# Perceiver block: pairs of batches for the last channels, one S step, and the tail column by DMA

## The reference

```
q, k, v = x@Wq, ctx@Wk, ctx@Wv           # 8 heads of 64
x += softmax(q k^T / 8) v @ Wo + bo      # over the 257 context rows of the batch
w = sigmoid(xn@Wx@Ww + bw); k, v, r = xn@Wk, xn@Wv, sigmoid(xn@Wr)
state_t = (1 - w_t) state_{t-1} + k_t v_t^T;  out_t = r_t state_t   # 4 heads, 32 steps
x += out @ Wo
x += gelu(xn@U1@V1 + b1) @ U2 @ V2 + b2
```

## Time and profile before

| | |
|---|---|
| median of 3 runs | 970.15 us (969.84 to 971.87) |
| profiled execution | 969.11 us, span 967.1 us |
| PE busy | 943.9 us (98%) |
| ACT, DVE, POOL busy | 607.3, 613.0, 373.8 us |
| DMA | 79.03 MB, mean 82 GB/s |

### The profile page before, as it was taken

The page is one execution under the profiler, slowest core; times in us unless marked ns, Lnnn a source line. Parts: engine busy times, 40 slices in busy tenths (PEclk is TensorE's granted clock), DMA queues, the critical chain, the costliest instruction groups (busy, mean ns, idle before and its releaser), DMA issues.

```text
span 967.1 us, 23520 instructions
## 1 busy us (share of the span) xinstructions
PE 943.9 (98%) x9012; PEld 783.6 (81%) x9012; DVE 613.0 (63%) x1286; ACT 607.3 (63%) x1487; POOL 373.8 (39%) x484
## 2 busy tenths in 40 slices
PE   9999999999999999999999999999999999999998
PEld 7767888787888878798887878888787888877775
DVE  4765858476685847668485666747567584746461
ACT  3545657667575766767576675757757566674533
POOL 1423534244352524435253352524326252433330
PEclk9999999999999999999999999999999999999999
DMA  8314231322323132132222313122222313222000
GB/s 304 120 51 124 59 105 49 100 81 65 105 78 90 51 101 81 60 110 61 88 69 87 95 60 94 60 87 89 81 80 81 90 49 89 87 73 72 9 12 22
DMA packets 58013, 79.03 MB, mean 82 GB/s; under 512 B 10288, under 2 KB 39856, under 8 KB 57904
## 3 DMA queue, kind: packets, MB, share of 16 engines
q1 hardware_dynamic: 56192, 76.38, 25.9%
q10 hardware_dynamic: 1712, 1.16, 0.4%
HBM read 73.05 MB, written 4.46 MB: 80 GB/s over the span
## 4 chain that ended last, share of the span: by engine, by line
PE 78%; DVE 9%; ACT 7%; issue 3%; POOL 1%; DMA 0%; DVEq 0%; POOLq 0%; ACTq 0%
PE gb L369 16%; PE scores L428 7%; PE acc L459 7%; PE gb L492 6%; PE acc L455 6%; PE scores L432 6%; PE ptp L442 5%; PE acc L460 5%; PE gb L613 3%; PE gb L602 3%; DVE xn L840 3%; ACT probs L685 3%; PE gb L401 3%; DVE probs L853 2%; DVE small L846 2%
## 5 line engine op out<-in xcount | busy, mean ns | idle before, releaser
L1100 POOL TENSOR_TENSOR t_l<-raw_t,t_h 128x516 fp32r<-128x516 f32 x128 | 167.5, 1309 | 193.6 <-PE scores L432 131.0
L685 ACT ACTIVATE probs<-scores,small 128x257 f32<-128x257 f32 x256 | 119.1, 471 | 134.6 <-DVE small L846 134.4
L846 DVE TENSOR_REDUCE small<-scores 128x2 f32<-128x514 f32 x128 | 88.3, 690 | 127.5 <-PE scores L432 127.4
L1109 POOL TENSOR_TENSOR ptm<-probs,head 128x32 f32<-128x32 f32 x128 | 35.1, 274 | 261.9 <-DVE probs L853 261.9
L853 DVE TENSOR_TENSOR probs<-probs,small 128x514 f32<-128x514 f32 x128 | 101.7, 794 | 4.4
L459 PE MATMUL acc<-pt,raw_n 128*128 128x256 f32 x256 | 89.6, 431 | 0.0
L442 PE MATMUL ptp<-ident,probs 128*128 128x128 f32 x512 | 78.7, 276 | 10.5 <-DVE probs L853 9.4
L696 ACT ACTIVATE pt<-ptp 128x512 f32<-128x512 f32 x128 | 77.2, 603 | 13.2 <-PE ptp L442 11.7
L455 PE MATMUL acc<-pt,raw_n 128*64 128x128 f32 x1024 | 82.7, 282 | 2.3 <-ACT pt L696 0.4
L428 PE MATMUL scores<-t_h,qk_h 128*128 128x258 f32 x256 | 83.3, 325 | 0.0
L455 PEld LDWEIGHTS acc<-pt,raw_n 128*64 128x64 f32 x1024 | 55.4, 136 | 31.9 <-issue 21.0
(11 more groups left out here) (178 smaller groups left out, 2768.8 us busy)
## 6 DMA issues: line engine op xcount, KB each, us to landing
raw_t<-in_ctx_t SPq DMA_DIRECT2D x128, 258.0 KB, 3.3
raw_n<-in_ctx_n SPq DMA_DIRECT2D x128, 192.0 KB, 2.4
xb<-in_x SPq DMA_DIRECT2D x16, 256.0 KB, 4.3
vsp<-tail_values SPq DMA_DIRECT2D x256, 2.0 KB
out<-ob SPq DMA_DIRECT2D x16, 256.0 KB, 2.9
xin<-in_x SPq DMA_DIRECT2D x15, 256.0 KB, 2.9
khat<-in_wq ACTq DMA_DIRECT2D x1, 512.0 KB, 4.3
wv<-in_wv SPq DMA_DIRECT2D x1, 512.0 KB, 6.3
```

Of the source, the lines that this page charges most:

```text
L685: go(probs[n % 2][:, r, 0:L], scores[:, r, 0:L], ACT.Exp, bias=nmax[:, r:r + 1], accum_out=rsum[:, r:r + 1]).then_inc(s["exp_ready"], 1)
L846: v_.tensor_reduce(nmax[:], scores[:, :, 0:L], AX.X, ALU.max, negate=True)\
L1100: p_.tensor_tensor(t_l[m % 2][:], raw_t[m % RING][:], t_h[m % 2][:].bitcast(F32), ALU.subtract)\
```

## The change

- pv: the 64-channel products of a batch are done by table RESTS: those of batches 2 and 3 both at b=3, 4 and 5 at b=5, 6 and 7 at b=7. At b=2, 4, 6 only L459 and L460 are left. The transposed probabilities of the first of each pair wait in `xn0`'s memory (`pt_late`), so step xn0 waits for the group's last sums. `pc_out` copies 256 columns for such a batch and 128 more for its partner. `raw_n` loads of a pair come together.
- Tail column: POOL's `ptm`, PE's TP and DVE's `psp` product go. SP moves the last column of each half by a DMA (128 numbers on 128 partitions to 4 rows of 32) into one of two zeroed `psp`, so two DMAs a batch; ACT's exps wait for those of two batches before. Half of the `vsp` DMAs go.
- S is one step with two tiles at b=7 instead of two steps with four; DVE has two masks of twice the size, behind `norm_probs`.
- Order of the fills: Qf from b=0 to b=7 (same group, one batch earlier), H from b=7 to b=6, Pf from b=6 to b=4, v from b=6 to b=5, Y3 from b=1 to b=2.

```diff
-FILL1 = [["Sq", "Qf", "WV"], ["O2"], [], ["Qa0"], ["Qa1"], ["Qb"], [], ["Sp", "H0", "H2"]]
-FILL2 = [["St"], ["Y3", "Y1", "XT"], ["Y2", "XT2", "q0", "q2"], ["z", "q1", "q3", "XT3"], ["k"], ["r"], ["Pf", "v"],
-         ["TP"]]
+FILL1 = [["WV"], ["O2"], [], ["Qa0"], ["Qa1"], ["Qb"], ["H0", "H2"], ["S", "Qf"]]
+FILL2 = [["St"], ["Y1", "XT"], ["Y3", "Y2", "XT2", "q0", "q2"], ["z", "q1", "q3", "XT3"], ["k", "Pf"], ["r", "v"], [],
+         []]
+RESTS = [[0], [1], [], [2, 3], [], [4, 5], [], [6, 7]]
...
-SHIFT = {"XT": PREP, "TP": HERE}
+TILES.update({"S": ["S0", "S1"], "St": ["St0", "St1"]})
+SHIFT = {"XT": PREP}
 SHIFT.update({f"q{p}": PREP for p in range(4)})
 SHIFT.update({n: PREP for n in ("Qa0", "Qa1", "Qb")})
-SHIFT.update({n: POST for n in "WV Y1 XT2 z k r v Sp".split()})
-SHIFT.update({n: FFN for n in "Sq St O2 Y2 XT3 Pf H0 H2".split()})
-SHIFT.update({n: END for n in ("Qf", "Y3")})
+SHIFT.update({n: POST for n in "WV Y1 XT2 z k r v S".split()})
+SHIFT.update({n: FFN for n in "St O2 Y2 XT3 Pf H0 H2 Qf".split()})
+SHIFT["Y3"] = END
...
+def rests(n):
+    return [n - n % G + b for b in RESTS[n % G]]
+def sums(n):
+    return sum(1 + 2 * len(rests(m)) for m in range(n + 1))
...
+        pt_late = xn0[:].rearrange("p t d -> p (t d)").rearrange("p (t m) -> p t m", t=LT)
...
+        def pt_of(n):
+            return pt if n in rests(n) else pt_late
...
+                    step = n - RING
+                    while n - RING not in rests(step):
+                        step += 1
+                    sp.wait_ge(s["acc_ready"], sums(step))
...
-                    for half in range(2):
-                        sp.dma_start(vsp[half * 64 + h:half * 64 + 64:H, cols], scratch[g * G:(g + 1) * G, cols])\
-                            .then_inc(vsp_in, 16)
+                    half = h // 4
+                    sp.dma_start(vsp[half * 64 + h:half * 64 + 64:H, cols], scratch[g * G:(g + 1) * G, cols])\
+                        .then_inc(vsp_in, 16)
...
+            def tail_column(n):
+                g, b = n // G, n % G
+                if n == 0:
+                    sp.wait_ge(s["psp_ready"], 1)
+                sp.wait_ge(s["probs_ready"], n + 1)
+                if b == 0 and g > 1:
+                    bank, k = BANK["WV1", g - 2]
+                    sp.wait_ge(bank_filled[bank], k)
+                for r in range(2):
+                    row = 64 * r + H * b + 4 * r
+                    sp.dma_start(psp[g % 2][row:row + 4, b], probs[n % 2][:, r, L - 1:L]).then_inc(tail_in[n % 2], 16)
...
+                for m in rests(n):
+                    c0 = P * (n - m)
+                    for t in range(LT):
+                        for k in range(2):
+                            last = mm(acc[64 * k:64 * k + 64, 1, c0:c0 + P], raw_n[m % RING][:, t, P:C],
+                                      pt_of(m)[:, t, k * P:(k + 1) * P], start=t == 0, stop=t == 1)
+                            if t == 1:
+                                last.then_inc(s["acc_ready"], 1)
+                x, p_ = raw_n[n % RING], pt_of(n)
+                mm(acc[:, 0], x[:, 0, 0:P], p_[:, 0], start=True, stop=False)
+                mm(acc[:, 0], x[:, 1, 0:P], p_[:, 1], start=False, stop=True).then_inc(s["acc_ready"], 1)
...
+            def s_tiles(g):
+                even, odd = (tile(n, g)[:].rearrange("p a (c k) -> p (a c) k", k=P) for n in ("S0", "S1"))
                 pe.wait_ge(s["hat_ready"], HATS * (g + 1))
                 pe.wait_ge(s["rhat_ready"], 2 * (g + 1))
                 for t in range(2):
-                    t_ = slice(t * P, (t + 1) * P)
-                    for i in range(NB):
-                        keys = i * 2 * T + c * T + t * P
-                        queries = i * 2 * T // NB + (2 * c + t) * 32
-                        for r0, out_ in ((0, even), (64, odd)):
-                            last = mm(out_[32 * i:32 * i + 32, 0, t_],
-                                      rhat[r0:r0 + 64, queries:queries + 32],
-                                      khat[r0:r0 + 64, keys:keys + P], start=True, stop=True)
-                            if (t, i) == (1, NB - 1):
-                                done(f"S{2 * c + r0 // 64}", g, last)
+                    for c in range(2):
+                        for i in range(NB):
+                            keys = i * 2 * T + c * T + t * P
+                            queries = i * 2 * T // NB + (2 * c + t) * 32
+                            for r0, out_ in ((0, even), (64, odd)):
+                                last = mm(out_[32 * i:32 * i + 32, 2 * t + c], rhat[r0:r0 + 64, queries:queries + 32],
+                                          khat[r0:r0 + 64, keys:keys + P], start=True, stop=True)
+                                if (t, c, i) == (1, 1, NB - 1):
+                                    done(f"S{r0 // 64}", g, last)
...
-                    act.wait_ge(s["ptm_ready"], n - 1)
+                    act.wait_ge(tail_in[n % 2], 32 * (n // 2))
...
+                act.wait_ge(s["acc_ready"], sums(n))
+                b, own = n % G, n in rests(n)
+                if len(rests(n)) > 1:
+                    go(pc[:, H:, (b - 1) * S:b * S], acc[:, 1, P:2 * P].rearrange("p (h s) -> p h s", s=S), ACT.Copy)
+                columns = H + H // 2 if own else H
+                go(pc[:, 0:columns, b * S:(b + 1) * S],
+                   acc[:].rearrange("p c (h s) -> p (c h) s", h=H)[:, 0:columns], ACT.Copy)\
...
-                    drain(n, g, v_.copy_predicated(s_q[:, 2 * c + e:2 * c + e + 5:4],
-                                                   mask[:].rearrange("p (o q) -> p o q", o=1).to_broadcast([P, 2, P]),
-                                                   t[:, 0].rearrange("p (t q) -> p t q", t=2)))
+                    drain(n, g, v_.copy_predicated(s_q[:, int(n[1])::2],
+                                                   mask[:].rearrange("p (o q) -> p o q", o=1).to_broadcast([P, 4, P]),
+                                                   t[:].rearrange("p a (c q) -> p (a c) q", q=P)))
...
-            GAPS = [[["psp-1"], ["S2-2", "S3-2"], ["WV0-1", "WV1-1"]],
-                    [[], [], ["O2-2", "Y3-3", "Y1-1"]],
-                    [["XT+1", "xn1-1"], [], []],
+            GAPS = [[[], [], ["WV0-1", "WV1-1"]],
+                    [[], [], ["O2-2", "Y1-1"]],
+                    [["XT+1", "xn1-1"], [], ["Y3-3"]],
                     [["Y2-2"], ["XT2-1", "xn2-2"], ["Qa0+1"]],
                     [[], ["su-1"], ["Qa1+1", "ti-1", "i0-1"]],
-                    [[], ["cf-1"], ["Qb+1", "i1-1"]],
-                    [[], ["i2-1", "pr-1"], ["rh-1", "ln0+2"]],
-                    [[], ["S0-1", "S1-1"], ["xn0+2"]]]
-            AT_END = [[[["psp-1"], ["S2-2", "S3-2"], ["WV0-1", "WV1-1"]],
+                    [[], ["cf-1"], ["Qb+1", "i1-1", "i2-1"]],
+                    [[], ["pr-1"], ["rh-1", "ln0+2"]],
+                    [[], [], ["S0-1", "S1-1", "xn0+2"]]]
```

More of the change, by code:

```diff
@@ L181, in build @@
         pc = sb("pc", [P, H + H // 2, T])
-        ptm = [sb(f"ptm{i}", [P, 2, 2, G, H]) for i in range(2)]
-        psp = sb("psp", [P, G, S])
-        ones = psp[:].rearrange("p b s -> p (b s)")
+        psp = [sb(f"psp{i}", [P, G, S]) for i in range(2)]
+        zeros = psp[1][:].rearrange("p b s -> p (b s)")
         vsp = sb("vsp", [P, INNER])
         xin, xn0 = sb("xin", [P, 2, D]), sb("xn0", [P, 2, D])
+        pt_late = xn0[:].rearrange("p t d -> p (t d)").rearrange("p (t m) -> p t m", t=LT)
         hid = sb("hid", [P, 8, T])
@@ L250, in build @@
                              "out_done"))
+        tail_in = [sem(f"tail_in{i}") for i in range(2)]
         ctxt_in = [sem(f"ctxt_in{i}") for i in range(RING)]
@@ L450, in pv @@
                     pe.wait_ge(s["pc_ready"], n)
-                x = raw_n[n % RING]
-                for t in range(LT):
-                    for k in range(2):
-                        last = mm(acc[64 * k:64 * k + 64, 1, 0:P], x[:, t, P:C], pt[:, t, k * P:(k + 1) * P],
-                                  start=t == 0, stop=t == 1)
-                        if t == 1:
-                            last.then_inc(s["acc_ready"], 1)
-                mm(acc[:, 0], x[:, 0, 0:P], pt[:, 0], start=True, stop=False)
-                mm(acc[:, 0], x[:, 1, 0:P], pt[:, 1], start=False, stop=True).then_inc(s["acc_ready"], 1)
+                for m in rests(n):
+                    c0 = P * (n - m)
[8 more added lines that the diff above has]
+                mm(acc[:, 0], x[:, 1, 0:P], p_[:, 1], start=False, stop=True).then_inc(s["acc_ready"], 1)
             def tail_values():
@@ L477, in wz_product @@
                 done("WZ", 0, last)
-            def turn_tails(g):
-                out_ = tile("TP", g)
-                pe.wait_ge(s["ptm_ready"], (g + 1) * G)
-                for r in range(2):
-                    last = mm(out_[:, 0, 0:S], ptm[g % 2][:, r].rearrange("p a b h -> p (a b h)"), diag[:],
-                              start=r == 0, stop=r == 1)
-                done("TP", g, last)
```

(9 more changed lines are left out.)

92 lines of the change are left out of this document (38 added, 54 removed).

## The result

The changed kernel takes 987.26 us (median of 4 runs, 985.8 to 988.14), the kernel before 970.76 in the same comparison (4 runs, 969.84 to 971.87): a ratio of 1.0168, 95% interval 1.0150 to 1.0186. It is slower by 16.5 us. The forecast was 971.0 with a range of 957 to 980; the time lies outside it.

What follows compares the result with a forecast made beforehand. PE, busy for 98% of the span, was taken to bound the kernel. Steady groups -1.3, borders +1.0, +2.3 and -1.6, small DMAs +1.1: +1.5 us on the profiled 969.1, given as 971 us, range 957 to 980.

Steps and rivals of the forecast that it cites:

- v, Pf, Y3, Qf, H change place and keep their length: On PE in a steady group: the moved steps take as long as before, 0.68 + 1.60 for Pf and v, 1.78 for Qf.
- Y3 now stands behind the sums of b=2 as cover: At b=2: Y3 fills PE's wait for the normalized probabilities, 0.15 us, part of the 0.5 of idle time.
- ACT's stretch: H's gelus and two table loads: next exps 9.35 us after L432 of score(7), so PE waits 1.35 at b=7.
- The pairs: Last 64 channels of two batches in one section: saving 0.15 x 3 = 0.45 us of PE a group.
- PE's work fell by 1.0: PE's work in a steady group: 1.0 us less, beside 0.5 less waiting.
- TP and S: On PE in a group: dropping the tail transposes saves 0.37 us; S in one step, with its new neighbours, 0.2.
- Idle time at b=2, b=6 and in H: PE's short waits at these places in a group go, saving 0.5 us.
- The masks behind the normalization: DVE's masks of S, about 1.3 us, end before the next maximum and cost nothing, within some tenths.
- The small DMAs: Tail column on SP's queue, 0.6 us an issue: hidden in steady groups, +1.1 us once in iteration 0.
- The borders: Outside the steady groups: iteration 1 +1.0 us, iteration 2 +2.3, iteration 15 and the ending -1.6, iteration 0 +1.1.
- v's copy does wait for i2: Rival at b=5: the copy, ahead of exps(7), starts ACT's stretch later; 0.4 us gives 977 us; chance 0.15.
- The gap at b=7: Rival: PE's wait at transpose(8) is hidden, a group gains up to 1.5 us, about 955 us; chance 0.2.

Runs made afterwards that it cites:

- the run with the old order: The changed kernel with the fill order, Qf's shift and Y3's add as before the change; pairs, one-step S with late masks and small DMAs kept: 1001.49 us.
- the early add: The changed kernel, but DVE adds Y3 at b=2 between the maximum and the product of the probabilities instead of behind the product: 970.63 us, ratio 1.0000.

## Why the prediction was wrong

- **The step that failed**: "v, Pf, Y3, Qf, H change place and keep their length", with "Y3 now stands behind the sums of b=2 as cover". Y3 keeps its length, but it moved on DVE too, behind the normalization, while the step that wants its bank came nearer. Its drain then freed the bank late, and PE's product for the queries waited 1.28 us in each of twelve groups. The prediction has no term for that wait: it counted PE's work and ACT's stretch and didn't go round the four banks. Its price is 1.42 us x 12 = 17.0, the whole miss: without it the kernel takes 970.63, the forecast 971.0. It was no rival either.
- **ACT's stretch**: right, 9.38 for 9.35, and the run without table loads shows that it decides b=7.
- **The pairs**: "Saving 0.15 x 3 = 0.45" was too large. In the steady group of the new order they save 0.08 of its time and nothing of PE's work: PE is busy for 55.7 us of a group with pairs and for 55.55 without. L491's busy time in the changed kernel is 71.5 us against 82.7 for L455, so 11 less for "some 7", but busy times overlap with those of the neighbours on PE and aren't time won. That PE's work fell by 1.0 as forecast is in part luck: the rest of the change, without pairs, takes off nearly 1.2, where 0.57 was forecast for TP and S. So the group came close (56.9 for 56.78 with the early add) by terms that are wrong one by one.
- **Idle time at b=2, b=6 and in H**: put at 0.5 and gone with the early add, but a group of the kernel before had only 0.3 us of it. A single product at b=2 was free before Y3 came there and costs 0.43 after.
- **The masks behind the normalization** were put at nothing: right in this order, 12 x 1.5 us and more in the old one.
- **The small DMAs**: hidden, as forecast; the cost in iteration 0, +1.1, was 1.3 at its b=7. The rule of the Trainium skill, "DMA: Bandwidth & Descriptors", section "Rules for kernel authors", on one descriptor per element shows in the packets (41600 under 512 B, before 10288; 256 DMAs of 128 elements are 32768), not in the time.
- **The borders**: iteration 2 +2.1 for +2.3. Iteration 1 is +2.45 for +1.0; about 1.2 of it is a fall of the clock (below), since in the kernel with Y3's add and the masks early, which has no fall there, the iteration takes 51.02, so +1.2. Iteration 15 with the ending -1.0 for -1.6, and the start and iteration 0 +2.35 for +1.1. Together the borders are +5.9 where +2.8 was forecast. In the kernel with the early add they are +5.2 (a span of 968.8, so +1.7, and 3.5 won in the twelve groups, where 1.3 was forecast): two misses that hide each other, so that its 970.6 lies so near the forecast 971.0 is luck. Why the first transpose starts anywhere from 24.9 to 25.65 in kernels that don't differ up to there, I can't explain.
- **The rivals**: none of the three came true. v's copy does wait for i2 (15 times, 5.6 us), but b=5 and b=6 are as long as forecast. The gap at b=7 isn't hidden, and the small DMAs aren't late.

## What to carry to other kernels

When a step is moved in an order in which buffers go round, follow its buffer: which step gets it next, and where in its engine's order stands the instruction that frees it. A drain behind an instruction that waits for a third engine can cost more than the whole change earns, here 17 us by one entry of a table. What a cover is worth changes with what stands in it already: the same product at b=2 was free in one order and cost 0.43 in another. A saving in the steady groups (pairs, 0.08 a group) can be lost at the borders (1.0 and 2.2 us, once, about half of the second the clock).

## What the runs showed of the hardware

TensorE's granted clock fell in the middle of the program, from 2.4 to 1.2 GHz for 3.4 us, in the changed kernel once, at b=7 of iteration 1, just after this transpose (in the two stretches of 5 us below it the third number from the right, 0.84 and 0.81, is the mean granted clock as a share of 2.4 GHz):

```profile
117.36 0.66 PE L477 MATMUL ptp<-ident,probs 128*128 128x128 f32 x4 [1.92 <-DVE probs L886]
```

```profile
115.00:120.00 5.00, 3.08 (x34) 2.21 (x40) 4.14 (x12) 2.42 (x7) 1.88 (x2) 0.84 0.33 70
120.00:125.00 5.00, 5.00 (x96) 4.16 (x80) 3.42 (x7) 2.12 (x8) 1.28 (x2) 0.81 0.16 47
```

In the run with the old order it fell five times, four of them in the batches b=7 of 10.65 us, where 9.02 is the rule: 1.6 us for each fall. PE had been idle for 1.9 us before H in each of these; but the same idle time in the other nine groups and one of 1.98 us in iteration 0 of the changed kernel brought no fall. The fifth fall came after 1.86 us of idle time at b=2 of iteration 15; 1.86 us at the same place of the kernel before brought none. The kernel before and the one without pairs in the new order have no fall in the whole span of their traces; the latter's longest idle time after iteration 0's start is 1.6 us. The spread between runs of one kernel is of this size too: of the 25 runs of the kernel before that stand beside the one without pairs in the new order, nine with a mean granted clock of 1.0 have a median of 969.73 us and thirteen with 0.998 one of 971.30. So a wait can cost nearly twice what it lasts, but not each time, and what decides between them the runs don't show.
